# A fused decoder layer on one core: context and weights of the cross attention in fp32r parts, key and query stacks per group of four heads

## The chip, the cores and the metric

One Trainium2 chip, one of its cores. The metric is device time in microseconds (us) of one execution, lower is better. The kernel before took 1267.0 us (median of 3 runs, 1264.37 to 1269.11).

## What is computed

A batch of B = 8 sequences of T = 512 positions, width D = 256, float32. Three sublayers, each followed by a residual sum and a layer norm:

```python
x = _layernorm(x + _L0_attn_ref(x, ...))        # linear attention with decay 0.99, memory of 128
x = _layernorm(x + _L0_xattn_ref(x, ctx, ...))  # q from x; k, v from the context; 16 heads of 16, softmax
x = _layernorm(x + _L0_ffn_ref(x, ...))         # self attention, 16 heads, softmax, plus the experts:
# attn_out + moe_out
gate = _softmax(x @ W_gate + b_gate)            # 8 experts, the 2 largest gates kept, the others 0
expert_out = einsum('bsd,edf->bsef', x, W_experts) + b_experts
moe_out = einsum('bsef,bse->bsf', expert_out, combine)
```

## The kernel before

Both softmax attentions run through one pipeline. It passes over 16 phases: "C" (cross) and "S" (self) of the eight sequences, in the order C0, C1, S0, C2, S1 ... C7, S6, S7 (`PHASES`). A phase has four groups of four heads, so there are 64 groups, g = 0 to 63. A group takes four slots (one for each block of 128 keys), and a slot has two halves (one for each pair of heads). Slot s, half h is written (s, h) in the tables and step t = 2s + h in the loops. In a half-slot TensorE issues: the score matmuls of two heads (PSUM tile sc), two tiles whose row maxima are wanted six slots ahead (mx), in h = 0 the products of probabilities and values of the slot before (op), and in h = 1 what the tables put there, called units. ScalarE takes exp(sc) to probs, VectorE reduces each mx tile to maxima.

The row maxima come into the scores through two extra rows of the query stack: when a group's 16 max tiles are reduced, VectorE makes shift_n, TensorE transposes it (unit `shift`, in slot 4g-2, h = 1), VectorE copies it to shift_r, and SyncE (SP) sends two small DMAs `qs<-shift_r` into the stack (`shift(g)`, step 2(4g-2)+1). The first scores of the group, in slot 4g, wait for them on `shift_in`.

A stack (tiles ks and qs) holds three copies of a head's 16 rows (high, high, low parts against high, low, high). The `high` and `low` of a projection are the fp32r value and the rest: ScalarE writes the one, VectorE (`low`) the other into k_parts or q_parts. SP then sends six DMAs per stack (`stack`, L399), 128 KB each: one stack is half a phase (two groups, `HALF` = 4 heads deep on each side), in a ring of `RING` = 3. SP takes its DMAs in the order of the table OTHERS["sp"], each after its own waits, so a DMA that waits holds up all behind it.

Units go through two PSUM banks of tile ms, in turn: a unit may start only when the unit before the last one has been read out of its bank (`unit`, `wait_unit_out(pe, *ORDER[u - 2])`). For kc, qc, k3c, q3c it is VectorE's `low` that frees the bank, for `shift` the copy to shift_r, for most others a copy of ScalarE. The tables LIN_* place the units of the first two sublayers relative to the start of the C phase (kc0, kc1: keys of the context, two chunks; cv0, cv1: its values; qc: queries), MID_* those of the rest (k3c, q3c, v3a, v3b; x2T; gate; combT: transposes of the gates; be0, be1: gates times expert biases), MOE_* the 16 expert products. `heads` transposes a finished group's output in slot 4g+6, h = 1.

kc and cv are plain float32 products on ctxT_s, which SP loads whole into a tile of its own (L385). be0 and be1 are float32 products of combT (8 rows, kept in o1T) with the biases. k3c, q3c, v3 and the experts are already made from fp32r parts: three products (high by high, low by high, high by low) in one PSUM sum (`project_parts`, `project_part_rows`). The experts' results go ScalarE -> moe -> GpSimd, which adds them into x2.

Before the pipeline starts there are 23 slots of preparation for sequence 0 and 1 (LIN_FIRST, LIN_SECOND); the order of the queues there is written out at the start of each engine's block.

## Time and profile before

| | us |
|---|---|
| median of 3 runs | 1267.0 |
| the profiled execution's own time | 1266.94 |
| its span, first to last instruction | 1265.0 |
| TensorE matmul busy | 1220.8 (96%) |
| VectorE busy | 902.8 (71%) |
| ScalarE busy | 771.1 (61%) |
| GpSimd busy | 366.0 (29%) |

Matmuls are pipelined, so a busy time of TensorE adds up overlapping instructions and shows that it had work, not that it ran at its peak; what a unit costs is read from its start to the start of what follows. A float32 matmul stands in the trace as two instructions, an fp32r matmul as one. The steady part is the same from sequence to sequence, with a period of 149.3 us (two phases, 32 slots).

### The profile page before, as it was taken

The numbers are of one execution on the slowest core, as the hardware profiler recorded it, in microseconds if no ns is written. First come the engines' busy times: TensorE is split into PE (matmuls) and PEld (weight loads), VectorE is DVE, ScalarE is ACT, GpSimd is POOL, SyncE is SP. The second block draws the span as 40 slices with busy tenths as digits, with TensorE's granted clock in tenths as the row PEclk, the third lists the DMA queues.
The fourth block names the chain that finished last, engine by engine and source line by source line (L and its number), as shares of the span: only waits on it lengthen the run. The fifth ranks groups of instructions, "written<-read, shape, count | busy, mean of one in ns | idle before, by whom it ended". The sixth has DMA issues, their size and how long they took to land.

```text
span 1265.0 us, 19962 instructions
## 1 busy us (share of the span) xinstructions
PE 1220.8 (96%) x6936; PEld 601.8 (48%) x6936; DVE 902.8 (71%) x1836; ACT 771.1 (61%) x1072; POOL 366.0 (29%) x471
## 2 busy tenths in 40 slices
PE   8889999999999999999999999999999999999998
PEld 4433444544555445454554545454454534544443
DVE  2577886677777787777776777767877787667772
ACT  2255556666675765756657665666657576655664
POOL 6410103211621134320522206221153204430261
PEclk9899999999999999999999999999999999999999
DMA  7825034313233342233333143332223333303300
GB/s 254 135 43 94 18 52 68 51 29 76 50 69 52 51 85 42 51 45 70 68 67 61 20 74 68 68 52 45 51 42 51 52 52 52 68 2 52 52 19 18
DMA packets 50243, 74.92 MB, mean 59 GB/s; under 512 B 8536, under 2 KB 20320, under 8 KB 49888
## 3 DMA queue, kind: packets, MB, share of 16 engines
q1 hardware_dynamic: 48896, 72.72, 32.8%
q10 hardware_dynamic: 1248, 0.92, 0.4%
q8 instruction: 57, 0.93, 0.4%
q14 instruction: 42, 0.34, 0.1%
HBM read 18.04 MB, written 4.19 MB: 18 GB/s over the span
## 4 chain that ended last, share of the span: by engine, by line
PE 83%; DVE 7%; ACT 5%; issue 3%; DMA 1%; ACTq 0%; POOL 0%; SPq 0%; DVEq 0%
PE ms L451 38%; PE op L451 17%; PE sc L451 15%; PE mx L451 9%; DVE maxes L928 3%; ACT probs L759 2%; PE ms L557 2%; PE ms L502 1%; ACT moe L752 1%; PE ms L552 1%; DMA qs<-q_parts 1%; DMA w_ident<-in_ident 1%; DVE k_parts L838 0%; ACT x L777 0%; DVE heads L901 0%
## 5 line engine op out<-in xcount | busy, mean ns | idle before, releaser
L928 DVE TENSOR_REDUCE maxes<-mx 128x1 f32<-128x512 f32 x1024 | 657.4, 683 | 215.3 <-PE mx L451 213.4
L759 ACT ACTIVATE probs<-sc 128x1024 f32<-128x1024 f32 x512 | 524.3, 1024 | 373.8 <-PE sc L451 368.3
L1131 POOL TENSOR_TENSOR x<-x,moe 128x256 f32<-128x256 f32 x256 | 187.4, 732 | 687.0 <-ACT moe L752 666.5
L451 PE MATMUL op<-probs,v 128*32 128x512 f32 x2048 | 273.6, 606 | 2.9 <-ACT oT L697 2.5
L451 PE MATMUL sc<-qs,ks 50*128 50x512 f32 x1024 | 256.7, 497 | 11.9 <-ACT probs L759 10.3
L451 PEld LDWEIGHTS sc<-qs,ks 50*128 50x128 f32 x1024 | 95.4, 183 | 308.4 <-ACT probs L759 231.5
L451 PE MATMUL mx<-ks,qs 48*128 48x512 f32 x1024 | 209.0, 402 | 10.9 <-DVE maxes L928 8.9
L752 ACT ACTIVATE moe<-ms,comb 128x256 f32<-128x256 f32 x256 | 106.8, 472 | 22.1 <-PE ms L451 22.1
L451 PEld LDWEIGHTS mx<-ks,qs 48*128 48x128 f32 x1024 | 97.7, 187 | 20.8 <-DVE maxes L928 14.7
L451 PE MATMUL ms<-we_hi,x2T_hi 128*128 128x512 f32 x256 | 93.7, 447 | 2.5 <-DVE shift_r L892 1.3
L451 PEld LDWEIGHTS op<-probs,v 128*32 128x32 f32 x2048 | 40.5, 108 | 96.4 <-issue 95.0
L451 PE MATMUL ms<-we_hi,x2T_lo 128*128 128x512 f32 x256 | 80.5, 396 | 0.0
L451 PE MATMUL ms<-we_lo,x2T_hi 128*128 128x512 f32 x256 | 80.3, 394 | 0.0
L451 PEld LDWEIGHTS ms<-we_hi,x2T_hi 128*128 128x128 f32 x256 | 39.1, 188 | 35.4 <-issue 18.8
L451 PEld LDWEIGHTS ms<-we_lo,x2T_hi 128*128 128x128 f32 x256 | 48.0, 188 | 11.8
L451 PEld LDWEIGHTS ms<-we_hi,x2T_lo 128*128 128x128 f32 x256 | 48.0, 188 | 11.7
L838 DVE SCALAR_TENSOR_TENSOR k_parts<-ms,w_bk,k_parts 128x512 fp32r<-128x512 f32 x32 | 24.0, 751 | 33.7 <-ACT k_parts L698 33.3
L1093 POOL TENSOR_SCALAR var<-mv 128x4 f32<-128x4 f32 x24 | 5.5, 230 | 125.8 <-DVE mv L959 110.7
L557 PE MATMUL ms<-w_ident,oT 128*128 128x128 f32 x256 | 39.9, 279 | 1.8 <-DVE shift_r L892 1.0
L698 ACT ACTIVATE k_parts<-ms,w_bk 128x512 fp32r<-128x512 f32 x32 | 22.0, 687 | 32.1 <-PE ms L451 27.3
L844 DVE TENSOR_TENSOR v<-ms,w_bv 128x512 f32<-128x512 f32 x32 | 22.1, 690 | 27.2 <-PE ms L451 27.2
L557 PEld LDWEIGHTS ms<-w_ident,oT 128*128 128x128 f32 x256 | 29.5, 140 | 20.3 <-DVE shift_r L892 14.5
(131 smaller groups left out, 1264.8 us busy)
## 6 DMA issues: line engine op xcount, KB each, us to landing
ks<-k_parts SPq DMA_DIRECT2D x192, 128.0 KB, 4.2
qs<-q_parts SPq DMA_DIRECT2D x189, 128.0 KB, 4.6
xT_s<-in_xT SPq DMA_DIRECT2D x8, 512.0 KB, 3.8
x_s<-in_x SPq DMA_DIRECT2D x8, 512.0 KB, 4.0
ctxT_s<-in_ctxT SPq DMA_DIRECT2D x8, 512.0 KB, 4.2
out<-x SPq DMA_DIRECT2D x7, 512.0 KB, 2.9
qs<-shift_r SPq DMA_DIRECT2D x128, 8.0 KB
probs<-in_we SPq DMA_DIRECT2D x1, 1024.0 KB, 7.1
```

What stands on the lines that cost most here:

```text
L451: return nc.tensor.matmul(dst, lhsT, rhs, start=first, stop=last, skip_group_check=True)
L502: last = nc.tensor.transpose(bank[:, t * P:(t + 1) * P], src[:, t, c * P:(c + 1) * P], ident[:])
L552: last = nc.tensor.transpose(bank[0:SHIFT * HG * TB, 0:P], shift_n[:, n % 2].rearrange("p s a m -> p (s a m)"), ident[:])
L557: last = nc.tensor.transpose(bank[:, t * P:t * P + P], oT[:, t * P:t * P + P], ident[:])
L698: return nc.scalar.activation(dst, src, ACT.Identity, bias=bias, scale=1.0)
L752: nc.scalar.activation(moe[:, k % 2, j * D:j * D + D], bank[:, j * D:j * D + D], ACT.Copy, scale=comb[:, t, e:e + 1]).then_inc(moe_out, 1)
L759: nc.scalar.activation(probs[:, (2 * s + h) % 3, :, :], sc[:], ACT.Exp).then_inc(exp_out, 1)
L838: nc.vector.scalar_tensor_tensor(out=part[name][:, 1, :].bitcast(F32R), in0=unit_bank((task, n)), scalar=bias[:, c:c + 1], in1=part[name][ ...
L844: return nc.vector.tensor_tensor(dst[:, 2 * h:2 * h + 2, 0:H * VW].rearrange("p n (h d) -> p n h d", h=H)[:, :, :, 0:HD], unit_bank((task, ...
L928: nc.vector.tensor_reduce(maxes[:, g % 2, at:at + 1], mx[:, i % 3, :], AX_X, ALU.max).then_inc(max_out, 1)
L1093: nc.gpsimd.tensor_scalar(var[:, k, :], mv[:, k, :, 1], EPS, None, ALU.add).then_inc(step, 1)
L1131: nc.gpsimd.tensor_tensor(x2[:, n % 2, t, :], x2[:, n % 2, t, :], moe[:, k % 2, j * D:j * D + D], ALU.add).then_inc(acc, 1)
```

## The change

1. Keys and values of the cross attention are made of fp32r parts. The context comes raw into x1 (sequences 0 and 1) or x_s (from 2 on), ScalarE writes its high part (`ctx_high`), GpSimd the low one (`ctx_low`; for sequence 0 VectorE, `first_lows`). The weights wk2 and wv2 are loaded into x1b and split the same way at the start. kc0 and qc0 change places from sequence 2 on; kc0 of sequence 1 comes a slot earlier. The load of x for the next sequence goes behind `ctx_low`.
2. Stacks are per group: DMAs of half the size and twice as many, in a ring of five groups, and a semaphore for even and for odd groups. The second group's stack is issued at its own place in SP's order.
3. The expert bias is one fp32r product with 24 rows: VectorE builds comb3 (high, low, high parts of the gates; three more instructions in `choose_end`), and combT goes from (33, 1) to (34, 0) for sequences 1 to 6.
4. To make room: the value tiles v2 have 17 columns per head in place of 20, and above and tied lie in moe.

```diff
-VW = HD + 4
+VW = HD + 1
 SHIFT = 2
 SIDES = 2
-PAIRS = H // SIDES
-HALF = PAIRS // DC
-RING = 3
+WIDE = HG // SIDES
+RING = 5
...
-             "x1": (-16, 0), "qc0": (-15, 0), "cv1": (-15, 1), "kc1": (-14, 1), "qc1": (-7, 1),
+             "x1": (-16, 0), "qc0": (-15, 0), "cv1": (-15, 1), "kc1": (-14, 1), "qc1": (-6, 1),
...
-              "o1": (-2, 1), "y01": (-1, 1), "y23": (0, 1), "kc0": (2, 1), "x0": (4, 0), "x1": (5, 0), "qc0": (6, 1),
+              "o1": (-2, 1), "y01": (-1, 1), "y23": (0, 1), "kc0": (1, 1), "x0": (4, 0), "x1": (5, 0), "qc0": (6, 1),
...
-              "x_bias": (-4, 0), "x1_bias": (20, 1), "load_xT": (-4, 0), "load_x": (3, 0), "load_ctx": (12, 0)}
+              "x_bias": (-4, 0), "x1_bias": (20, 1), "load_xT": (-4, 0), "load_x": (3, 0), "load_ctx": (-15, 0),
+              "ctx_high": (-12, 1), "ctx_low": (-3, 0)}
...
-       "o1": (-23, 1), "y01": (-21, 0), "y23": (-20, 0), "x0": (-16, 0), "x1": (-15, 0), "kc0": (-14, 0),
-       "qc0": (-13, 1), "cv0": (-9, 1), "cv1": (-8, 1), "kc1": (-6, 0), "qc1": (-5, 1),
+       "o1": (-23, 1), "y01": (-21, 0), "y23": (-20, 0), "x0": (-16, 0), "x1": (-15, 0), "qc0": (-14, 0),
+       "kc0": (-13, 1), "cv0": (-9, 1), "cv1": (-8, 1), "kc1": (-6, 0), "qc1": (-5, 1),
...
-       "x_bias": (-27, 0), "x1_bias": (7, 0), "load_xT": (-31, 0), "load_x": (-17, 1), "load_ctx": (-1, 0)}
+       "x_bias": (-27, 0), "x1_bias": (7, 0), "load_xT": (-31, 0), "load_x": (-14, 1), "load_ctx": (-17, 1),
+       "ctx_high": (-15, 0), "ctx_low": (-15, 0)}
...
-            "gate": (29, 0), "gateT": (31, 0), "combT": (33, 1), "be0": (36, 0), "be1": (37, 0), "k3c0": (34, 0), "q3c0": (35, 1),
+            "gate": (29, 0), "gateT": (31, 0), "combT": (34, 0), "be0": (36, 0), "be1": (37, 0), "k3c0": (34, 0), "q3c0": (35, 1),
...
+        if n >= 1:
+            halves["sp"][lin_at("load_ctx", n)].append(("load_ctx", n))
+            halves["act"][lin_at("ctx_high", n)].append(("ctx_high", 0, n))
+            halves["pool"][lin_at("ctx_low", n)].append(("ctx_low", 0, n))
...
-                    halves["sp"][at(f"{name}{c}", n) + 1].append(("stack_" + kind, 2 * PHASE[layer, n] + c))
+                    t, g = at(f"{name}{c}", n), 4 * PHASE[layer, n] + 2 * c
+                    halves["sp"][t + 1].append(("stack_" + kind, g))
+                    halves["sp"][max(t + 1, 2 * 4 * (g + 1 - RING + 1) + 2) if g >= RING else t + 1].append(("stack_" + kind, g + 1))
...
-        ctxT_s = sb("ctxT_s", [P, DC, T])
+        ctxT_part = (sb("ctxT_hi", [P, DC, T]), sb("ctxT_lo", [P, DC, T]))
+        w2_part = {name: (sb(name + "_hi", [P, DC, D]), sb(name + "_lo", [P, DC, D])) for name in ("wk2", "wv2")}
...
+        comb3 = sb("comb3", [P, TB, TERMS * E])
+        be_part = sb("be_part", [TERMS * E, D])
+        be_stage = moe[0:TERMS * E, 1, 0:D]
...
+        def ctx_stage(n):
+
+            return (x1 if n < 2 else x_s)[:].rearrange("p n d -> p (n d)").rearrange("p (c t) -> p c t", c=DC)
...
+                    if n == 1:
+                        wait_unit(sp, "x0", 0)
+                        wait_unit(sp, "x1", 0)
+                        sp.wait_ge(x1b_out, TB)
+                    elif n >= 2:
+                        sp.wait_ge(ln_out[0], TB * (n + 1))
+                    sp.dma_start(ctx_stage(n), ctxT[n:n + 1].rearrange("o (c p) t -> p (o c) t", p=P)).then_inc(ctx_in, 16)
+
+            def stack(name, g):
...
+                first = 32 * (g % 2)
+                sp.wait_ge(part_low[name], g // 2 + 1)
+                if g == 0:
                     sp.wait_ge(fills, 5)
-                if e >= RING:
-                    sp.wait_ge(score, 2 * 8 * (e - RING + 1))
-                    sp.wait_ge(max_t, 32 * (e - RING + 1))
-                for side in range(SIDES if (name, e) != ("q", 0) else 1):
+                if g >= RING:
+                    sp.wait_ge(score, 2 * TB * (g - RING + 1))
+                    sp.wait_ge(max_t, HG * TB * (g - RING + 1))
+                for side in range(SIDES if (name, g) != ("q", 0) else 1):
                     for r in range(TERMS):
                         at = 64 * side + HD * r
-                        sp.dma_start(dst[at:at + HD, e % RING, :, :],
-                                     part[name][64 * side:64 * side + 64, which[r], :]).then_inc(stack_in[name], 16)
+                        src = 64 * side + first
+                        sp.dma_start(dst[at:at + HD, g % RING, :, :],
+                                     part[name][src:src + 32, which[r], :]).then_inc(stack_in[name][g % 2], 16)
...
-                    last = project(bank, W["wk2"], ctxT_s, slice(c * P, c * P + P))
+                    pe.wait_ge(ctx_low, DC * (n + 1))
+                    if n == 0:
+                        pe.wait_ge(w2_low, 2)
+                    last = project_parts(bank, w2_part["wk2"], ctxT_part, slice(c * P, c * P + P))
...
-                    last = project_rows(bank, D, ctxT_s, W["wv2"], slice(0, D), (2 * h, 2 * h + 1))
+                    pe.wait_ge(ctx_low, DC * (n + 1))
+                    if n == 0:
+                        pe.wait_ge(w2_low, 2)
+                    last = project_part_rows(bank, D, ctxT_part, w2_part["wv2"], slice(0, D), (2 * h, 2 * h + 1))
...
-                        last = nc.tensor.transpose(bank[0:E, t * P:t * P + P], comb[:, t, :], ident[:])
+                        last = nc.tensor.transpose(bank[0:TERMS * E, t * P:t * P + P], comb3[:, t, :], ident[:])
...
-                        last = mm(bank[:, j * D:j * D + D], combT[:, t * P:t * P + P], W["be"][:], True, True)
+                        last = mm(bank[:, j * D:j * D + D], combT[:, t * P:t * P + P].bitcast(F32R), be_part[:].bitcast(F32R),
+                                  True, True)
...
+            def context_high(n):
+                act.wait_ge(ctx_in, 16 * (n + 1))
+                if n >= 1:
+                    wait_unit(act, "kc1", n - 1)
+                    wait_unit(act, "cv1", n - 1)
+                for c in range(DC):
+                    copy(ctxT_part[0][:, c, :].bitcast(F32R), ctx_stage(n)[:, c, :]).then_inc(ctx_high, 1)
...
+                if t == lin_at("s23", 0):
+                    act.wait_ge(w2_in, 16 * 2)
+                    for name in w2_part:
+                        copy(w2_part[name][0][:].bitcast(F32R), w2_stage[name]).then_inc(w2_high, 1)
+                    context_high(0)
...
+            def first_lows():
+
+                for k, name in enumerate(w2_part):
+                    dve.wait_ge(w2_high, k + 1)
+                    nc.vector.tensor_tensor(w2_part[name][1][:].bitcast(F32R), w2_stage[name], w2_part[name][0][:],
+                                            ALU.subtract).then_inc(w2_low, 1)
+                for c in range(DC):
+                    dve.wait_ge(ctx_high, c + 1)
+                    nc.vector.tensor_tensor(ctxT_part[1][:, c, :].bitcast(F32R), ctx_stage(0)[:, c, :], ctxT_part[0][:, c, :],
+                                            ALU.subtract).then_inc(ctx_low, 1)
+
...
+                g_wait(COMB_STEP)
+                if n >= 1:
+                    wait_unit(dve, "combT", n - 1)
+                nc.vector.tensor_copy(comb3[:, :, 0:E].bitcast(F32R), comb[:]).then_inc(g_step, 1)
+                g_wait(COMB_STEP + 1)
+                nc.vector.tensor_tensor(comb3[:, :, E:2 * E].bitcast(F32R), comb[:], comb3[:, :, 0:E],
+                                        ALU.subtract).then_inc(g_step, 1)
+                nc.vector.tensor_copy(comb3[:, :, 2 * E:3 * E].bitcast(F32R), comb3[:, :, 0:E]).then_inc(g_step, 1)
...
+                elif task == "ctx_low":
+                    for c in range(DC):
+                        pool.wait_ge(ctx_high, DC * n + c + 1)
+                        nc.gpsimd.tensor_tensor(ctxT_part[1][:, c, :].bitcast(F32R), ctx_stage(n)[:, c, :], ctxT_part[0][:, c, :],
+                                                ALU.subtract).then_inc(ctx_low, 1)
```

Where it moves instructions. First TensorE, sequence 3, slots 33 and 34 relative to the start of its C phase. Before (comb is the transposes of unit combT, shift_n those of shift, oT those of heads, x2T_hi with w_hi the first part of k3c0):

```order
L451 MATMUL ms<-we_lo,x2T_hi 128x512 x2
L594 MATMUL ms<-w_ident,comb 8x128 x4
...
L552 MATMUL ms<-w_ident,shift_n 32x128
L451 MATMUL ms<-x2T_hi,w_hi 128x512 x2
L451 MATMUL ms<-x2T_lo,w_hi 128x512 x2
L451 MATMUL ms<-x2T_hi,w_lo 128x512 x2
L557 MATMUL ms<-w_ident,oT 128x128 x4
L451 MATMUL sc<-qs,ks 128x512 x2
```

and in the changed kernel:

```order
L473 MATMUL ms<-we_lo,x2T_hi 128x512 x2
...
L578 MATMUL ms<-w_ident,shift_n 32x128
L473 MATMUL ms<-x2T_hi,w_hi 128x512 x2
L473 MATMUL ms<-x2T_lo,w_hi 128x512 x2
L473 MATMUL ms<-x2T_hi,w_lo 128x512 x2
L620 MATMUL ms<-w_ident,comb 24x128 x4
L583 MATMUL ms<-w_ident,oT 128x128 x4
L473 MATMUL sc<-qs,ks 128x512 x2
```

combT now stands between k3c0 and heads, so the unit before the last one of heads is k3c0; before it was shift.

Second SP's queue around the second `shift` (group 1) at the start of the pipeline. Before:

```order
L376 DMA xT_s<-in_xT 128x2x512
L410 DMA qs<-shift_r 2x8x128 x4
L380 DMA x_s<-in_x 128x4x256
L399 DMA ks<-k_parts 16x4x512 x6
L410 DMA qs<-shift_r 2x8x128 x2
```

and in the changed kernel:

```order
L390 DMA xT_s<-in_xT 128x2x512
L429 DMA qs<-shift_r 2x8x128 x2
L420 DMA ks<-k_parts 16x2x512 x12
L429 DMA qs<-shift_r 2x8x128 x2
L396 DMA x_s<-in_x 128x4x256
```

The key stacks of groups 4 and 5 stand ahead of the shift of group 1; that of group 5 waits until all scores of group 0 are made.

Third SP's queue ahead of the shift of the first group of a C phase, here C2 (group 12; key and query stacks of groups 14 and 15, from kc1 and qc1 of sequence 2). Before:

```order
L399 DMA ks<-k_parts 16x4x512 x6
L399 DMA qs<-q_parts 16x4x512 x6
L410 DMA qs<-shift_r 2x8x128 x2
```

and in the changed kernel:

```order
L420 DMA ks<-k_parts 16x2x512 x6
L420 DMA qs<-q_parts 16x2x512 x6
L420 DMA ks<-k_parts 16x2x512 x6
L420 DMA qs<-q_parts 16x2x512 x6
L429 DMA qs<-shift_r 2x8x128 x2
```

From the query parts of qc1 on, 18 DMAs of stacks stand ahead of the shift in place of six.

## Rows read from the trace of the kernel before

**Rows 1.** The windows view, one steady period (busy us of each engine, granted clock)

```profile
432.59:581.93 149.34, 148.49 (x862) 73.71 (x862) 111.79 (x228) 95.95 (x135) 43.43 (x58) 1.00 0.34 58
```

**Rows 2.** Timeline of TensorE, units cv0 and kc1 (start us, us, line, operation)

```profile
557.85 1.89 PE L451 MATMUL ms<-w_wv,ctxT_s 128*128 128x256 f32 x8
559.67 0.50 PE L451 MATMUL sc<-qs,ks 50*128 50x512 f32 x2
...
571.70 1.88 PE L451 MATMUL ms<-ctxT_s,w_wk 128*128 128x512 f32 x4
...
573.42 0.60 PE L557 MATMUL ms<-w_ident,oT 128*128 128x128 f32 x4
```

**Rows 3.** The same view, q3c0 (from parts), be0, and two pieces of v3a

```profile
314.01 0.62 PE L451 MATMUL ms<-x2T_hi,w_hi 128*128 128x512 f32 x2
...
315.50 0.50 PE L451 MATMUL sc<-qs,ks 50*128 50x512 f32 x2
...
317.83 1.13 PE L451 MATMUL ms<-w_be,o1T 8*128 8x256 f32 x4
318.89 0.73 PE L451 MATMUL ms<-we_hi,x2T_hi 128*128 128x512 f32 x2
...
329.01 0.40 PE L451 MATMUL ms<-w_hi,x2T_lo 128*128 128x256 f32 x2
329.25 0.40 PE L451 MATMUL ms<-w_lo,x2T_hi 128*128 128x256 f32 x2
```

**Rows 4.** Timeline of all engines, slots 33 and 34 of sequence 3 (last: idle, releaser)

```profile
603.57 0.60 PE L594 MATMUL ms<-w_ident,comb 128*8 128x128 f32 x4
...
606.89 0.72 PE L451 MATMUL ms<-x2T_hi,w_hi 128*128 128x512 f32 x2 [0.17 <-ACT o1T L697]
...
608.40 0.60 PE L557 MATMUL ms<-w_ident,oT 128*128 128x128 f32 x4
...
608.66 0.69 ACT L698 ACTIVATE k_parts<-ms,w_bk 128x512 fp32r<-128x512 f32 x1 [0.91 <-PE ms L451]
...
609.38 0.75 DVE L838 SCALAR_TENSOR_TENSOR k_parts<-ms,w_bk,k_parts 128x512 fp32r<-128x512 f32 x1 [1.39 <-ACT k_parts L698]
```

**Rows 5.** The tile and source views: SP's time for one DMA (min/median/max ns)

```profile
L399 SPq DMA_DIRECT2D ks<-k_parts x192: 547/597/1104, 27.4 to 1178.2; - x192
...
L410 SPq DMA_DIRECT2D qs<-shift_r x128: 610/636/717, 62.9 to 1236.5; - x128
```

**Rows 6.** Timeline: query stack of qc1, and the scores that the next shift feeds

```profile
581.90 3.97 SPq L399 DMA_DIRECT2D qs<-q_parts  x6
...
595.11 0.50 PE L451 MATMUL sc<-qs,ks 50*128 50x512 f32 x2
```

**Rows 7.** The same at the start of C7 (group 52), with the shift

```profile
1029.83 3.75 SPq L399 DMA_DIRECT2D qs<-q_parts  x6
...
1037.85 16.30 SPq L410 DMA_DIRECT2D qs<-shift_r  x4
...
1040.60 0.50 PE L451 MATMUL sc<-qs,ks 50*128 50x512 f32 x2 [0.75 <-DMA qs<-shift_r]
```

**Rows 8.** The same at groups 6 and 60

```profile
164.37 3.75 SPq L399 DMA_DIRECT2D qs<-q_parts  x6
...
176.49 0.50 PE L451 MATMUL sc<-qs,ks 50*128 50x512 f32 x2
...
1179.58 3.75 SPq L399 DMA_DIRECT2D qs<-q_parts  x6
...
1192.48 0.50 PE L451 MATMUL sc<-qs,ks 50*128 50x512 f32 x2
```

**Rows 9.** Timeline of TensorE: last scores of group 0, first of group 1

```profile
81.62 0.50 PE L451 MATMUL sc<-qs,ks 50*128 50x512 f32 x2
...
84.22 0.51 PE L451 MATMUL sc<-qs,ks 50*128 50x512 f32 x2
```

**Rows 10.** Windows: after the thin start, and around the wait of rows 7

```profile
74.00:79.00 5.00, 4.63 (x19) 1.42 (x18) 3.27 (x8) 3.40 (x5) 1.49 (x4) 0.66 0.01 3
...
1030.00:1060.00 30.00, 27.22 (x191) 12.60 (x195) 25.00 (x55) 19.14 (x27) 4.50 (x5) 1.00 0.31 48
```

**Rows 11.** Timeline of TensorE: the first max tiles

```profile
43.11 0.50 PE L451 MATMUL mx<-ks,qs 48*128 48x512 f32 x2 [2.01 <-DMA qs<-q_parts]
```

**Rows 12.** The page's groups: weight loads of the value products

```profile
L451 PEld LDWEIGHTS op<-probs,v 128*32 128x32 f32 x2048 | 40.5, 108 | 96.4 <-issue 95.0
```

More of the change, by code:

```diff
@@ L265, in decoder @@
         o1T = sb("o1T", [P, T])
-        combT = o1T[0:E, :]
+        combT = sb("combT", [TERMS * E, T])[:]
         gateT = sb("gateT", [P, P])[:]
@@ L272, in decoder @@
         part = {n: sb(n + "_parts", [P, 2, T]) for n in "qk"}
-        qs = sb("qs", [P, RING, HALF, T])
-        ks = sb("ks", [P, RING, HALF, T])
+        qs = sb("qs", [P, RING, WIDE, T])
+        ks = sb("ks", [P, RING, WIDE, T])
         v2 = [sb(f"v2_{n}", [P, TB, H * VW + 32 - VW]) for n in range(2)]
@@ L295, in decoder @@
         g_p = sb("g_p", [P, TB, E])
-        above = sb("above", [P, TB, E, E])
-        tied = sb("tied", [P, TB, E, E])
         rank = sb("rank", [P, TB, E])
@@ L300, in decoder @@
         moe = sb("moe", [P, 2, 512])
+        above, tied = (moe[:, 0, k * TB * E * E:(k + 1) * TB * E * E].rearrange("p (n e f) -> p n e f", n=TB, e=E) for k in range(2))
+        comb3 = sb("comb3", [P, TB, TERMS * E])
+        be_part = sb("be_part", [TERMS * E, D])
+        be_stage = moe[0:TERMS * E, 1, 0:D]
         we_part = (sb("we_hi", [P, DC, E * D]), sb("we_lo", [P, DC, E * D]))
@@ L305, in decoder @@
         W3_COLS = (slice(0, 2 * D), slice(2 * D, 3 * D))
+        w2_stage = {name: x1b[:, 2 * k:2 * k + 2, :] for k, name in enumerate(w2_part)}
         we_stage = (probs[:].rearrange("p s h t -> p (s h t)")[:, 0:E * D],
@@ L402, in shift @@
             def shift(g):
                 sp.wait_ge(shift_out, g + 1)
-                wide = HG // SIDES
-                first = wide * (g % 2)
                 for side in range(SIDES):
                     at = 64 * side + ROWS
-                    rows = SHIFT * wide * TB
-                    sp.dma_start(qs[at:at + SHIFT, stack_of(g) % RING, first:first + wide, :]
+                    rows = SHIFT * WIDE * TB
+                    sp.dma_start(qs[at:at + SHIFT, g % RING, :, :]
                                  .rearrange("a h (n t) -> a (h n) t", n=TB),
@@ L705, in high @@
                 if e >= 1:
-                    act.wait_ge(stack_in[name], 16 * TERMS * SIDES * e)
+                    for signal in stack_in[name]:
+                        act.wait_ge(signal, 16 * TERMS * SIDES * e)
                 wait_unit(act, task, n)
@@ L735, in take_out @@
                     wait_unit(act, task, n)
-                    copy(combT, bank[0:E, :]).then_inc(done, 1)
+                    copy(combT.bitcast(F32R), bank[0:TERMS * E, :]).then_inc(done, 1)
                 elif task in ("be0", "be1"):
@@ L770, in other @@
                         act.wait_ge(x1b_out, TB * n)
+                    if k == 0 and n < 2:
+                        act.wait_ge(ctx_low, DC * (n + 1))
                     if k == 1 and n == 0:
@@ L1053, in _ @@
                     dve.wait_ge(w3_cut, 4)
+                    dve.wait_ge(be_in, 16)
+                    nc.vector.tensor_copy(be_part[:].bitcast(F32R), be_stage).then_inc(be_cut, 1)
+                    dve.wait_ge(be_cut, 1)
+                    nc.vector.tensor_scalar(be_stage, be_stage, W["side"][:, 0:1], None, ALU.mult).then_inc(be_cut, 1)
+                    dve.wait_ge(be_cut, 2)
+                    nc.vector.scalar_tensor_tensor(out=be_part[:].bitcast(F32R), in0=be_part[:], scalar=W["side"][:, 1:2],
+                                                   in1=be_stage, op0=ALU.mult, op1=ALU.add).then_inc(be_cut, 1)
                 units = UNITS.get(t - 1, [])
@@ L1198 @@
         "we": by_chunk(arr(ffn + "W_experts").transpose(1, 0, 2).reshape(D, E * D)),
-        "be": arr(ffn + "b_experts"),
+        "be": np.tile(arr(ffn + "b_experts"), (TERMS, 1)),
+        "side": np.repeat(np.array([[0, 1], [0, 1], [1, -1]], np.float32), E, 0),
         "ident": np.eye(P, dtype=np.float32),
```

83 lines of the change are left out of this document (47 added, 36 removed).

## The prediction

> **What bounds the kernel now.** I read the windows of a steady period first. In 149.34 us TensorE has work for 148.49, VectorE for 111.79, ScalarE for 95.95, GpSimd for 43.43 [rows 1]. So TensorE's queue is the bound: what is taken out of it is won, and a wait put into it is lost, whatever the others do. Then I read its timeline for the price of the units that the change touches, the waits of the places where it moves something, and SP's queue, which is idle most of the time but feeds the scores of every group through `shift`. The sum is made against the profiled execution, 1266.94 us with a span of 1265.0, as good as the median of 1267.0. A measurement tells 0.5% (6.3 us) from no change: the bounds are 1260.7 and 1273.3.
>
> **Products from parts, less time.** A plain float32 kc takes 571.70 to 573.42, 1.72 us, a cv 557.85 to 559.67, 1.82 us [rows 2]. The like unit from parts, q3c0 (six instructions of 512 columns, the shape of the new kc), takes 314.01 to 315.50, 1.49 us. In v3a pairs of 256 columns start 0.24 apart (329.01, 329.25), so the new cv with 12 instructions takes 6 x 0.24 plus about 0.06, 1.50 us [rows 3]. That gives 0.23 per kc and 0.32 per cv, 1.1 us per sequence. For sequence 0 these units lie before the pipeline, under other waits, and I count nothing: 7 x 1.1 = 7.7 us. be0 now takes 317.83 to 318.89, 1.06 us [rows 3]; after it there are two instructions of 256 columns, 0.24 and some 0.1 of entry. 0.72 less, 16 times: 11.5 us. Together -19.2. combT's transposes keep their four instructions (24 columns are loaded in place of 8).
>
> The Trainium skill (FP8 and Floating Point Precision, TensorE Precision Notes) has true FP32 as four passes through the array, so kc from three products would take three quarters. By that a kc and a cv would save 0.43 to 0.46 instead of 0.23 and 0.32, 4.7 us more over seven sequences. The units of the same shape in this trace save less, and the rows decide.
>
> **Work on the other engines.** The split of the context costs ScalarE two copies and GpSimd two subtractions per sequence at slot -15; ScalarE has 53 us free in a period and GpSimd 106 [rows 1], and kc0 comes 2.5 slots (over 10 us) later. Nothing. If GpSimd's part were late, kc0 would wait on TensorE and all behind it; I leave that to the range. At the start, the added copies and subtractions fall into stretches in which ScalarE and VectorE wait for o1 and y01: nothing.
>
> **combT behind k3c0: a new wait.** Banks alternate, so heads waits until the unit before the last one has been read out. Before, that is shift, long read: heads follows k3c0 at 608.40 at once. Now it is k3c0, and its bank is free only when ScalarE has made the high part (608.66) and VectorE the low (609.38 plus 0.75 = 610.13) [rows 4]. The moves up to k3c0's end about cancel (combT's 0.6 and the 0.17 wait gone from before it, against VectorE's three more instructions in front of the max tiles), so k3c0 ends at about the same time as before, and heads starts at 610.2 in place of 608.40: +1.8 us. It stands in sequences 1 to 6: +10.8. Behind heads in TensorE's queue are the scores of the next slot, and nothing hides it.
>
> **Twice as many stack DMAs: shifts come late.** One stack DMA costs SP 0.6 us, a shift DMA of 8 KB 0.64 [rows 5]. The size makes no difference there, so I take 0.625 (3.75 for six) for the half-sized ones too. Ends: 0.3, if the cost went with the bytes, and 0.8 with an odd long one. The key and query stacks of a second half (kc1, qc1) now stand with 18 DMAs between the query's low part and the shift, before with six. 18 x 0.625 = 11.25, the shift's two 1.3, and its landing: at 1037.85 the shift was issued, ended by 1039.15, and the scores began at 1040.60 on it, so 1.4 [rows 7]. The scores can begin 13.95 us after the query stack's first DMA.
> - Group 28: 581.90 + 13.95 = 595.85 against 595.11 [rows 6]: 0.75 us. The same at the start of C2 to C6, five times: 3.7.
> - Group 52: 1029.83 + 13.95 = 1043.8 against 1040.60 [rows 7]: 3.2.
> - Groups 6 and 60: 178.3 against 176.49 and 1193.5 against 1192.48 [rows 8]: 1.8 and 1.0. Group 58 has the same queue as 6, and I take 1.8: together 4.6.
> - Group 1: the ring wait `if g >= RING` is not in the place of the stack of group 5 (g is 4 there), so SP waits with that stack until the last scores of group 0, at 81.62 plus 0.5, then six DMAs (3.75), the shift (1.3) and the landing (1.4): 88.6 against 84.22, of which cv0 is done 0.3 sooner [rows 9]: 4.7.
>
> Sum of shifts: 16.2 us, all in TensorE's queue.
>
> **Start.** The first max tile waits for q_parts at 43.11 [rows 11]. Its data are now half. On the other side the whole key stacks and a context load come ahead of it. I estimate 1.5 us less; ends 0 and 3.
>
> **Clock.** In 74 to 79 us the granted clock averages 0.66 of the full 2.4 GHz, so it was at its lower level of 1.2 GHz for most of it, after slots in which TensorE waited time and again; around a wait of 0.75 us in a dense part it stays at 1.00 [rows 10]. After the two long waits (4.7 and 3.2) I count a few us at half clock, 1.5 us together.
>
> The Trainium skill (TensorE: Matmul & The Clock Gate, Part 1) says that the throttled state is the default and activity releases it. That speaks against every wait that the change adds; with the long ones the trace agrees, with the short one not.
>
> **Sum.** -19.2 + 10.8 + 16.2 - 1.5 + 1.5 = +7.8 us, 1274.7 against the run of 1266.94: I forecast 1275, slower by 0.6%.
>
> **Rivals.**
> - **SP's issue goes with the size** (the other side). If a half-sized DMA costs 0.3 us, the 18 take 5.4 and all waits but that of group 1 are gone (it keeps 4.7 - 6 x 0.32 = 2.8). Sum -19.2 + 10.8 + 2.8 - 1.5 + 0.3 = -6.8: 1260, just faster. It decides below about 0.35 us per DMA. For it: nothing; against it: 8 KB and 128 KB cost the same [rows 5]. 0.12. Halfway (0.45) gives about 1264, no change: 0.05.
> - **The wait of heads is covered**: VectorE and ScalarE get to k3c0 sooner than rows 4 say, or the time comes back in the next slots. Then 1275 - 10.8 = 1264. TensorE has only 0.85 us without work in a period [rows 1], so I see no slack that could give it back. 0.20, no change.
> - **Shifts land later**, queued behind the stacks' data: two to three us more at each of ten places, 1295 at most, 1285 in the middle. For it: the transfers now stand directly ahead of the shift. Against: SP issues 64 KB in 0.625 us, half the rate of before. 0.13, slower.
> - **Value tiles of 17 columns**: the 2048 weight loads take 108 ns each [rows 12]. If the odd row width made each value product 5 ns longer, +10 us: 1285. No row shows it. 0.05, slower.
> - **Half clock after every wait**: ten waits, each with some 3 us of work at half speed, +1.5 us each, +13.5 beyond what is counted: 1288. Against it stands the short wait of rows 10. 0.05, slower. [...]
> - **Products at three quarters**: a kc or cv 0.2 or 0.14 us shorter than in rows 3, 1275 - 4.7 = 1270. Against: q3c0 has the shape. 0.02, no change. (So by the four passes of the Trainium skill, cited above.)
>
> **How the numbers follow.** The forecast has what is left, 0.38. With the three later cases (0.23) that is 0.61 for more than 1273.3 us; but the forecast lies only 1.7 us above that bound, and I give 0.11 of it to no change. Slower 0.50. No change: 0.11 + 0.20 + 0.05 + 0.02 = 0.38. Faster: 0.12. The 80% range goes from the first rival to the middle of the later ones: 1260 to 1286.
>
> **What would show it.** In the profile after: kc and cv units of 1.5 us, be of 0.35; SP's ks and qs issues still near 0.6 us, 384 and 381 of them; TensorE idle before heads' transposes, with VectorE's k_parts as releaser, 1 to 2 us, six times; score matmuls released by DMA qs<-shift_r, the longest at 84 to 89 us and at the start of C7; the steady period 149.3 - 1.1 - 1.4 + 1.8 + 0.75, near 149.3. Wrong if SP's issues are at 0.3 us, if heads does not wait, or if the period falls below 148.

## The result and the profile after

The changed kernel takes 1304.9 us, median of 4 runs (1301.7 to 1309.1), against 1267.8 before: ratio 1.0299, 95% interval 1.0262 to 1.0336, slower. The forecast was 1275 and the range ended at 1286: the direction was right, the size was off by 30 us. The profiled execution took 1306.02 us with a span of 1304.2, so it can be set against the span of 1265.0 before.

The page of the changed kernel: busy times, the granted clock in 40 slices, the chain that ended last by engine and by line, the groups of score and max matmuls with the idle time ahead of them, and the stack issues.

```profile
PE 1226.5 (94%) x7000; PEld 613.6 (47%) x7000; DVE 920.0 (71%) x1867; ACT 779.6 (60%) x1090; POOL 381.7 (29%) x485
...
PEclk9689998999999999999999999999999999999999
...
PE 71%; SPq 11%; DVE 7%; ACT 4%; issue 4%; DMA 3%; POOL 0%; ACTq 0%; DVEq 0%
...
L473 PE MATMUL sc<-qs,ks 50*128 50x512 f32 x1024 | 259.7, 503 | 34.6 <-DMA qs<-shift_r 22.9
```

SyncE's queue is now in the chain that ended last (SPq 11%), and the scores waited 22.9 us for the shift, 13 times; before it was one wait of 0.75 us. The views that answer to the forecast's sources, first the source views of SyncE's issues [rows 5] (min/median/max ns):

```profile
L420 SPq DMA_DIRECT2D ks<-k_parts x384: 558/592/1816, 27.4 to 1224.5; - x192
L420 SPq DMA_DIRECT2D qs<-q_parts x381: 558/592/1612, 37.2 to 1228.4; - x191
```

Half the bytes, the same 0.59 us at the median, as the forecast took it; single issues took up to 1.8 us. Then the timeline at group 28 [rows 6]: two issues of six stack DMAs and a third stand between the first query stack and the shift.

```profile
603.13 3.73 SPq L420 DMA_DIRECT2D qs<-q_parts  x6
606.97 4.44 SPq L420 DMA_DIRECT2D ks<-k_parts  x6
611.52 3.73 SPq L420 DMA_DIRECT2D qs<-q_parts  x6
615.30 1.32 SPq L429 DMA_DIRECT2D qs<-shift_r  x2
...
618.01 0.50 PE L473 MATMUL sc<-qs,ks 50*128 50x512 f32 x2 [1.59 <-DMA qs<-shift_r]
```

The shift lands 1.39 us after its issue has ended (616.62), as forecast. The two longest waits, of group 1 [rows 9] and of group 52 [rows 7], and the pieces of the first max tiles' timeline [rows 11]:

```profile
42.80 0.50 PE L473 MATMUL mx<-ks,qs 48*128 48x512 f32 x2 [4.26 <-DMA qs<-q_parts]
...
95.57 0.80 PE L473 MATMUL sc<-qs,ks 50*128 50x512 f32 x2 [3.59 <-DMA qs<-shift_r]
...
1071.57 0.79 PE L473 MATMUL sc<-qs,ks 50*128 50x512 f32 x2 [4.16 <-DMA qs<-shift_r]
```

Timeline at slot 34 of sequence 3 [rows 4]: heads' transposes wait for the low part of k3c0 and not for their own operand.

```profile
631.81 0.61 PE L620 MATMUL ms<-w_ident,comb 128*24 128x128 f32 x4
631.99 0.69 ACT L725 ACTIVATE k_parts<-ms,w_bk 128x512 fp32r<-128x512 f32 x1 [1.41 <-PE ms L473]
...
632.71 0.75 DVE L885 SCALAR_TENSOR_TENSOR k_parts<-ms,w_bk,k_parts 128x512 fp32r<-128x512 f32 x1 [0.95 <-ACT k_parts L725]
...
633.51 0.66 PE L583 MATMUL ms<-w_ident,oT 128*128 128x128 f32 x4 [1.10 <-DVE k_parts L885]
634.10 0.50 PE L473 MATMUL sc<-qs,ks 50*128 50x512 f32 x2
```

Windows of the changed kernel: the start, and the stretch behind the wait of group 52 (columns as in [rows 1]; the granted clock is the last but two).

```profile
44.00:68.00 24.00, 21.60 (x40) 9.45 (x40) 12.32 (x23) 3.24 (x6) 16.61 (x10) 0.51 0.44 110
...
1071.00:1082.00 11.00, 9.74 (x36) 3.60 (x37) 7.18 (x19) 4.70 (x6) 0.00 (x0) 0.53 0.01 2
```

TensorE has work for nine tenths of both and runs at its lower level of 1.2 GHz, called half clock below. Added up from the clock's record, it was there for 64.9 us of the execution, against 11.6 us before. The four runs of the changed kernel order themselves by it: 1309.1 us at a mean granted clock of 0.973, 1306.0 at 0.975, 1303.8 at 0.979, 1301.7 at 0.987.

**Where the time went.** I set the start of each group's first scores against before (after minus before, as steps from group to group):

| place | step, us | forecast |
|---|---|---|
| group 0, the start | +8.0 | -1.5 |
| groups 1 and 2 | +5.9 | +4.7 |
| groups 6 to 8 | +4.7 | +1.8 |
| groups 12, 20, 28, 36, 44 | +7.6 | +3.7 |
| groups 40, 48, 56 | +1.5 | 0 |
| slots 33 to 35, seen at groups 13, 21, ..., 53 | +16.7 | +10.8 |
| groups 52, 58 to 60 | +8.2 | +6.0 |
| all others, the shorter units | -13.5 | -19.2 |
| sum | +39.1 | +6.3 and 1.5 for the clock |

No place is new except groups 8, 40, 48 and 56; each term came out worse than forecast. What the experiments have to tell is why.

### The profile page after: what moved, and what is told of

It reads as the page before. It is cut to its first block, busy times and chain, and to the rows that moved or that the text cites. A ratio compares the mean times of both kernels' runs of the same rounds, so it can differ in the third digit from the quotient of the medians.

```text
span 1304.2 us, 20667 instructions
## 1 busy us (share of the span) xinstructions
PE 1226.5 (94%) x7000; PEld 613.6 (47%) x7000; DVE 920.0 (71%) x1867; ACT 779.6 (60%) x1090; POOL 381.7 (29%) x485
## 4 chain that ended last, share of the span: by engine, by line
PE 71%; SPq 11%; DVE 7%; ACT 4%; issue 4%; DMA 3%; POOL 0%; ACTq 0%; DVEq 0%
PE ms L473 31%; PE op L473 14%; PE sc L473 13%; SPq L420 10%; PE mx L473 8%; DVE maxes L975 3%; PE ms L583 2%; DMA qs<-shift_r 2%; PE ms L524 2%; ACT probs L789 1%; DVE q_parts L885 1%; ACT q_parts L725 1%; PE ms L578 1%; DVE k_parts L885 1%; SPq L429 1%
## 5 line engine op out<-in xcount | busy, mean ns | idle before, releaser
L473 PE MATMUL sc<-qs,ks 50*128 50x512 f32 x1024 | 259.7, 503 | 34.6 <-DMA qs<-shift_r 22.9
L473 PE MATMUL mx<-ks,qs 48*128 48x512 f32 x1024 | 213.6, 411 | 14.8 <-DVE maxes L975 10.5
L473 PEld LDWEIGHTS mx<-ks,qs 48*128 48x128 f32 x1024 | 100.4, 191 | 26.6 <-DVE maxes L975 13.5
L885 DVE SCALAR_TENSOR_TENSOR k_parts<-ms,w_bk,k_parts 128x512 fp32r<-128x512 f32 x32 | 24.0, 750 | 24.7 <-ACT k_parts L725 23.9
L724 ACT ACTIVATE oT<-op 128x512 f32<-128x512 f32 x64 | 38.3, 599 | 1.4 <-PE op L473 1.4
```

Source lines behind the costliest of these rows:

```text
L473: return nc.tensor.matmul(dst, lhsT, rhs, start=first, stop=last, skip_group_check=True)
L724: return nc.scalar.activation(dst, src, ACT.Copy)
L885: nc.vector.scalar_tensor_tensor(out=part[name][:, 1, :].bitcast(F32R), in0=unit_bank((task, n)), scalar=bias[:, c:c + 1], in1=part[name][ ...
```

## The experiments

Each edit is on the changed kernel unless said otherwise; kernel 5 is the kernel of run 5, and so on. Times are ratios to runs of the kernel before on the same chip; 1% is 12.7 us.

**1. qc1 back in its slot.**

```
-             "x1": (-16, 0), "qc0": (-15, 0), "cv1": (-15, 1), "kc1": (-14, 1), "qc1": (-6, 1),
+             "x1": (-16, 0), "qc0": (-15, 0), "cv1": (-15, 1), "kc1": (-14, 1), "qc1": (-7, 1),
```

> The changed kernel with the product qc1 of sequence 0 back in slot -7, ahead of the first max tiles, as before the change; nothing else. Theory (clock): the first scores are 8.0 us late because TensorE stood 4.3 us for the first stack, the granted clock fell and stayed at 0.5 for 23.9 us; with qc1 in the hole the wait falls to about 2 us, the half clock to about 7 us, the first scores come at 67 to 69 us, and the time is 1296 to 1300 us. Rival (queue): the stacks and the context load ahead on SyncE's queue make the start late whatever TensorE does; then the first scores stay at 73 to 75 us and the time at 1303 to 1306 us.

Measured: 1300.4 us, ratio 1.0239 (1.0216 to 1.0262). The wait of the first max tiles is 1.0 us, the half clock 6.8 us, the first scores stand at 69.15 us. That looks like the theory, but runs 3, 4 and 11 get to the same place without the edit (below), and run 12, which is run 3 with this edit added, is no faster than run 3 (1.0188 against 1.0179). What qc1 gains ahead of the first max tiles is lost behind them. ScalarE, VectorE and TensorE in this kernel:

```profile
44.77 1.14 ACT L724 ACTIVATE ctxT_hi<-x 128x512 fp32r<-128x512 f32 x2
45.81 0.68 ACT L725 ACTIVATE q_parts<-ms,bq2s 128x512 fp32r<-128x512 f32 x1
...
46.52 0.75 DVE L885 SCALAR_TENSOR_TENSOR q_parts<-ms,bq2s,q_parts 128x512 fp32r<-128x512 f32 x1 [1.23 <-ACT q_parts L725]
...
47.92 0.80 PE L473 MATMUL mx<-ks,qs 48*128 48x512 f32 x2 [2.04 <-DVE maxes L975]
```

The added copies of the context stand on ScalarE ahead of qc1's high part; VectorE waits 1.23 us for it with the max reductions queued behind, and TensorE 2.04 us for those.

**2. TensorE kept busy in front of the first max tiles.**

```
+                if s == -MAX_LEAD and h == 0:
+                    busy(5, T)
```

> The changed kernel with five filling products of 512 columns on TensorE just ahead of the first max tiles (about 4.3 us at full clock, the length of the wait there), qc1 left in slot -6. Theory (clock): the clock does not fall, or is back soon, the first scores come at 66 to 69 us, the time is 1296 to 1300 us. Rival (queue): first scores at 73 to 76 us, time 1303 to 1308 us. A third way: the place of qc1 behind the first max tiles costs by itself (its bank and ACT behind it), then the clock is full and the first scores are still later than 70 us.

Measured: 1300.7 us, ratio 1.0246 (1.0224 to 1.0267), first scores at 71.34 us. The clock fell all the same, 6.8 us, later. That is outside the ranges of both theories, and the first scores are later than in three of the four kernels without filling (68.76 to 74.82 us, below). Filling bought nothing that can be told from run 1, and the clock theory of the start has no support here.

**3. combT back in slot 33.**

```
-            "gate": (29, 0), "gateT": (31, 0), "combT": (34, 0), "be0": (36, 0), ...
+            "gate": (29, 0), "gateT": (31, 0), "combT": (33, 1), "be0": (36, 0), ...
```

> The changed kernel with the transpose of the combine weights back in slot 33 second half; nothing else. Theory (two banks): the heads unit waits no longer for the low part of k3c0, the 1.1 us waits go in all six middle sequences, and so does what follows them; time 6 to 11 us less than the changed kernel, 1294 to 1299 us. Rival (VectorE): the three more VectorE instructions at the end of the choice make the transpose itself wait in slot 33 for as long, and the step from slot 33 to 35 stays 2.3 to 2.9 us above before; time 1302 to 1305 us.

Measured: 1291.2 us, ratio 1.0179 (1.0155 to 1.0204), 1.2% off the changed kernel. Timeline of TensorE at the same slot:

```profile
617.98 0.60 PE L620 MATMUL ms<-w_ident,comb 128*24 128x128 f32 x4 [0.60 <-DVE comb L1115]
618.50 0.50 PE L473 MATMUL sc<-qs,ks 50*128 50x512 f32 x2
...
622.35 0.63 PE L473 MATMUL ms<-x2T_hi,w_lo 128*128 128x512 f32 x2
622.81 0.60 PE L583 MATMUL ms<-w_ident,oT 128*128 128x128 f32 x4
623.34 0.50 PE L473 MATMUL sc<-qs,ks 50*128 50x512 f32 x2
```

Both theories have a part. heads waits no longer, and the step at slots 33 to 35 falls by 1.73 to 2.36 us in five middle sequences and by 1.02 in the sixth. But the transpose now waits 0.60 us for VectorE's last combine instruction, and 0.52 to 0.55 us of the step stays (3.09 in the sixth, where the half clock of group 52's wait lies in it). The time fell by more than the 6 to 11 us expected: of the 15.2 us between the two profiles these steps are 11.0, and the start is 4.7.

**4. Odd groups' stacks behind the shift.** SyncE's queue alone:

```
-  ... max(t + 1, 2 * 4 * (g + 1 - RING + 1) + 2) if g >= RING else t + 1
+  ... max(t + 1, 2 * 4 * (g + 1 - RING + 1) + 6) if g + 1 >= RING else t + 1
```

> The changed kernel with the stacks of every odd group issued four half slots later, behind the shift that they stood ahead of, and group 5's stacks held to the same rule; nothing else. Theory (queue): the 13 waits of the scores for the shift (22.9 us in all) are the 0.62 us per issue of twelve stack transfers ahead of it; they fall under 3 us in all, and the half clock behind the two longest (groups 1 and 52) goes too; the time is 1274 to 1284 us. Rival (landing): the shift lands late since many small transfers are in flight, then the waits stay above 10 us in all and the time above 1292 us. Rival (buffers): the later stacks make ACT's copies of the next products wait for the stacks, the max tiles then wait for stacks, and the time stays above 1295 us with waits named after the parts.

Measured: 1288.6 us, ratio 1.0152 (1.0137 to 1.0167). All 13 waits for the shift are gone, so they were the queue. The time did not come down to the 1274 to 1284 us expected, because the load of the next context now stood behind those stacks. Timelines of SyncE, ScalarE and TensorE:

```profile
370.55 1.31 SPq L429 DMA_DIRECT2D qs<-shift_r  x2
371.98 4.25 SPq L420 DMA_DIRECT2D ks<-k_parts  x6
376.34 4.83 SPq L420 DMA_DIRECT2D qs<-q_parts  x6
381.21 0.58 SPq L404 DMA_DIRECT2D x_s<-in_ctxT  x1
...
385.19 1.15 ACT L724 ACTIVATE ctxT_hi<-x_s 128x512 fp32r<-128x512 f32 x2 [3.16 <-DMA x_s<-in_ctxT]
...
387.30 0.50 PE L473 MATMUL sc<-qs,ks 50*128 50x512 f32 x2 [3.17 <-ACT probs L789]
```

ScalarE waits for the context, the exponentials are queued behind that copy, and TensorE waits for them, in five periods (10.7 us in all). It is the same fault at another place: an urgent transfer behind twelve that have time.

Runs 3 and 4 leave the start as the changed kernel has it, and their first scores stand at 70.12 and 68.99 us, not at 74.82.

**5. All three edits** (runs 1, 3 and 4 together, the stacks five half slots later to pass the context's load).

> The changed kernel with all three edits at once: qc1 of sequence 0 back in slot -7, the transpose of the combine weights back in slot 33, and the odd groups' stacks behind the shift and behind the load of the next context (five half slots later than in the changed kernel, group 5's too). Theory (three added waits on top of a true saving): the ratios of the single edits add up (0.6%, 1.2%, 1.5% off 1.030), and the 13 us of waits for the context that the late stacks made are not there; the time is 1248 to 1258 us, below the kernel before by 1 to 1.6%. Rival (no saving): the cheaper products gave back their time elsewhere, and without the waits the time is that of before, 1265 to 1272 us.

Measured: 1282.6 us, ratio 1.0099 (1.0073 to 1.0125). A miss of both ranges: in the half slot that they now share, the stacks are still issued ahead of the load (11.4 us of waits for the context), and group 5's k stacks came so late that ScalarE waited for them (1.9 us, and 4.7 us at group 3).

**6. The expert bias in plain fp32 again**, on kernel 5.

```
-                        last = mm(bank[...], combT[:, t * P:t * P + P].bitcast(F32R), be_part[:].bitcast(F32R), True, True)
+                        last = mm(bank[...], combT[:, t * P:t * P + P], be_part[:], True, True)
```

> As the kernel with all three edits, with the expert bias's 16 x 2 products in plain fp32 again (over 24 rows, the same sum), nothing else. The prediction's price: 0.72 us per unit, 16 units, 11.5 us more than with all three edits. Rival (hidden): the units lie in slots that end on another engine, then it is 0 to 4 us.

Measured: 1284.5 us, ratio 1.0100 (1.0057 to 1.0143), 1.9 us above kernel 5 and not to be told from it: by time alone the rival's 0 to 4 us fits and the forecast's 11.5 does not. The timelines show what the unit itself does. With parts (kernel 5), and below it in fp32:

```profile
783.87 0.50 PE L473 MATMUL ms<-be_part,combT 24*128 24x256 f32 x2
784.30 1.13 PE L473 MATMUL ms<-x1T 128*128 128x512 f32 x2
```

```profile
785.97 1.13 PE L473 MATMUL ms<-be_part,combT 24*128 24x256 f32 x4
787.03 1.12 PE L473 MATMUL ms<-x1T 128*128 128x512 f32 x2
```

The unit takes 0.43 us in place of 1.06 [rows 3]; 0.63 us less where I had 0.72. Of it the scores show 0.40 us behind be0 and 0.48 behind be1 in sequences 1 to 5, 1.02 for both in sequence 6, 5.4 us together. So the term was too large; the time shows still less of it, and the waits for the context, which move the steps by up to 3.2 us at one place between these two profiles, hide how much.

**7. k and v of the context as one fp32 product of the high parts**, on kernel 5; it leaves out both products with low parts.

```
-                    last = project_parts(bank, w2_part["wk2"], ctxT_part, slice(c * P, c * P + P))
+                    last = project(bank, w2_part["wk2"][0], ctxT_part[0], slice(c * P, c * P + P))
```

and the like for v. 

> As the kernel with all three edits, with the products of k and v of the context as one plain fp32 product of the high parts, as many columns and as long as in the kernel before; it leaves out the two products with the low parts. The prediction's price: 0.23 us for each kc and 0.32 us for each cv unit, 7.7 us more than with all three edits (1.1 us per sequence). Rival (hidden): 0 to 2 us.

Measured: 1286.9 us, ratio 1.0125 (1.0076 to 1.0173). The intervals of 5 and 7 overlap (4.3 us between the medians, 7.7 forecast), but the steps of the scores are 0.30, 0.31, 0.30 and 0.31 us for the four units of a period, 1.2 us per sequence where I had 1.1. By the steps this term was right.

**8. The kernel before, with combT in slot 34**, and nothing else.

```
-            "gate": (29, 0), "gateT": (31, 0), "combT": (33, 1), "be0": (36, 0), ...
+            "gate": (29, 0), "gateT": (31, 0), "combT": (34, 0), "be0": (36, 0), ...
```

> The kernel before with one entry changed: the transpose of the combine weights in slot 34 first half, behind k3c0. Theory (two banks): the heads unit of slot 34 waits for k3c0's low part on VectorE, 1.1 us in each of the six middle sequences, and the scores of the slot behind it are 1.8 to 2.4 us later than before; time 7 to 14 us more than before. My prediction's own price was 1.8 us x 6 = 10.8 us. Rival: the wait is taken up by slack in the next slot, time within 3 us of before.

Measured: 1276.7 us, ratio 1.0044 (1.0021 to 1.0068), 5.6 us, a little under the 7 to 14 expected. The step is 1.25 to 1.29 us in five sequences and 1.48 in one, 7.8 us together. So moving the transpose alone costs 1.3 each, not my 1.8.

**9. The queue put right.** Kernel 5 with SyncE's order mended:

```
-  ... 2 * 4 * (g + 1 - RING + 1) + 7) if g + 1 >= RING else t + 1
+  ... 2 * 4 * (g + 1 - RING + 1) + (2 if g == 4 else 7 if g % 8 == 2 else 6)) if g + 1 >= RING else t + 1
+    for tasks in halves["sp"].values():
+        tasks.sort(key=lambda task: 0 if task[0] == "shift" else 1 if task[0] == "load_ctx" else 2)
```

> The changed kernel with qc1 of sequence 0 in slot -7, the combine transpose in slot 33, the odd groups' stacks behind the shift (group 5's in slot 5, the others' at least four half slots later than in the changed kernel), and the load of the next context ahead of the stacks of its half slot. Theory: what was left in the kernel with all three edits were waits of ScalarE for the context (1.5 to 3.2 us in each of five periods, 11.5 us in all) and for group 5's k stacks (4.7 us at group 3); both go, and the time is 1262 to 1268 us, 0 to 0.6% below before. Rival (landing): the context is waited for however early its load is issued, or the q stacks issued behind it are waited for instead; the time stays at 1275 to 1283 us.

Measured: 1263.3 us, ratio 0.9962 (0.9939 to 0.9984), as the theory has it: without its three added waits the change saves 0.4%. The timelines of SyncE at two places: shift ahead of the stacks, and the context ahead of them; then the windows view of the steady period.

```profile
589.17 1.31 SPq L431 DMA_DIRECT2D qs<-shift_r  x2
590.60 3.76 SPq L422 DMA_DIRECT2D ks<-k_parts  x6
594.47 3.74 SPq L422 DMA_DIRECT2D qs<-q_parts  x6
```

```profile
371.69 0.38 SPq L406 DMA_DIRECT2D x_s<-in_ctxT  x1
372.51 3.95 SPq L422 DMA_DIRECT2D ks<-k_parts  x6
```

```profile
410.63:558.32 147.69, 146.23 (x870) 73.68 (x869) 113.21 (x230) 96.68 (x136) 45.94 (x60) 1.00 0.24 59
```

A period of 147.7 us against 149.3 before and 151.1 in the changed kernel (slot 84 to slot 116, 488.30 to 639.43). No score waits for a shift, and no copy for a context. The half clock takes 18.0 us in all.

**10. The parts of the combine weights on GpSimd**, on kernel 9: the three instructions moved from VectorE.

```
-                nc.vector.tensor_copy(comb3[:, :, 0:E].bitcast(F32R), comb[:]).then_inc(g_step, 1)
+                    nc.gpsimd.tensor_copy(comb3[:, :, 0:E].bitcast(F32R), comb[:]).then_inc(g_step, 1)
...
```

> As the kernel just described, with the three parts of the combine weights made on GpSimd instead of VectorE. Theory (VectorE's order): the scores of slot 34 are 0.55 us later than before in each middle sequence because three more VectorE instructions (0.5 us) stand ahead of the max reductions; the step goes, 3 to 4 us less. Rival: GpSimd is slower and the transpose in slot 33 waits for it; 0 to 6 us more.

Measured: 1261.9 us, ratio 0.9954 (0.9929 to 0.9978), the same as kernel 9 by its interval. The step that it was to remove grew from 0.55 to 0.79 us, and the six waits of the transposes from 3.6 to 5.0 us in all, so my theory of it fell: it is the time until the combine weights are there that counts, and GpSimd is slower. Why the time is no worse stays open; the two kernels differ by half-clock pieces at other places.

**11. Only the condition for group 5.**

```
-  ... if g >= RING else t + 1
+  ... if g + 1 >= RING else t + 1
```

> The changed kernel with the condition of the stacks' place holding for group 5 too (its stacks in slot 5 instead of slot 2, behind shift 1); nothing else. Theory (ring): the 3.6 us wait of group 1's scores goes, and so does the half clock of some 7 us behind it (2.5 us at group 2); 5 to 6.5 us less than the changed kernel, 1298 to 1300 us. Its first part is the changed kernel's own, so its first scores are one more draw of the start: if 74.8 us belongs to the change they come at 73 to 76 us, if it was the clock's draw of one execution, at 69 to 71 us as in two of the kernels with other edits. Rival: the wait moves to group 2's shift, less than 2 us gained.

Measured: 1298.0 us, ratio 1.0251 (1.0204 to 1.0298). Group 1's wait falls from 3.59 to 1.25 us, and the steps of groups 1 and 2 by 3.8 and 2.8 us, 6.6 in all. The first scores stand at 68.76 us. In the changed kernel SyncE had issued both key stacks without a stop:

```profile
85.14 7.63 SPq L420 DMA_DIRECT2D ks<-k_parts  x12
```

So what the edit took away from in front of the shift was six issues; a standstill of SyncE for the ring does not show. The six of group 4's stack still stand there.

**12. Everything mended but the queue** (runs 1 and 3 together; it differs from kernel 9 in SyncE's order alone).

> The changed kernel with qc1 of sequence 0 in slot -7 and the combine transpose in slot 33, and SyncE's queue as in the changed kernel. It differs from the kernel of 1263 us in SyncE's order alone. Theory (the queue is the largest term): 12 to 13 waits of the scores for the shift, 19 to 23 us in all, and some us of half clock behind the longest; 1286 to 1291 us, 23 to 28 us above that kernel. The prediction's own price of the queue was 16.2 us, which would give 1279 to 1280 us. Rival (the edits overlap): the waits at the queue are partly the same time as the waits at the heads unit; then 1272 to 1279 us.

Measured: 1292.1 us, ratio 1.0188 (1.0161 to 1.0215), 2.26% or 28.7 us above kernel 9, just above the range. The waits for the shift are ten, 22.0 us in all. The two traces are 33.5 us apart (the profiled executions lie 2.1 us above and 2.7 below their medians), with 58.5 us at half clock against 18.0. The windows view from the first scores to the end, kernel 12 and then kernel 9:

```profile
68.78:1292.41 1223.63, 1167.32 (x6808) 581.69 (x6807) 886.04 (x1807) 760.41 (x1062) 346.24 (x454) 0.98 0.21 51
...
69.50:1258.89 1189.39, 1150.03 (x6808) 573.95 (x6807) 885.17 (x1807) 759.59 (x1062) 345.66 (x454) 1.00 0.22 53
```

Of the 34.2 us TensorE is idle for 17.0 (56.3 against 39.4) and busy for 17.3 more with the same 6808 matmuls. Idle time grows by less than the 22.0 us of waits for the shift, since other waits of TensorE (for maxima and combine weights) are shorter in kernel 12.

## Why the forecast was wrong

**What was right.** That TensorE's queue is the bound and little hides a wait in it; SyncE's 0.6 us per DMA, whether of 8, 64 or 128 KB; the landing of 1.4 us; group 5's stack ahead of the shift of group 1 (3.6 us of wait, 4.7 forecast); all the shift waits that were named; heads behind k3c0; k and v of the context (run 7). The rival "issue goes with the size" was rightly small, and value tiles of 17 columns cost nothing (weight loads 108 ns as in [rows 12]).

**The two terms that failed most are the shifts' 16.2 us and the clock's 1.5: together 17.7, and the queue cost 28.7 (run 12), 33.5 by the two traces.** The waits were forecast in the right places. Their steps add up to 21.2 us where I had 16.2, and groups 40, 48 and 56, which I did not name, add 1.5. Group 1 came out below its forecast (3.4 for 4.7) and group 52 near it (3.4 for 3.2; its wait of 4.16 us holds the 0.75 that it had before). The others were too small: 7.6 for 3.7 at the starts of C2 to C6, 2.3 and 3.2 for 1.8 at groups 6 and 58, 1.3 for 1.0 at group 60.

The step of the prediction that failed here is the queue's length, "18 x 0.625 = 11.25", and with it the 13.95 us from the first query stack to the scores. At groups 52 and 60, where every issue took 0.59 us, it was 14.2 us, for each change of tile costs 0.1. At the other ten places, where single issues took 0.7 to 1.6 us, it was 14.3 to 15.2 (14.88 at group 28: a stack of six took 4.44 us there). [rows 6] shows such a stack, 3.97 us for six, and I took 3.75. Where a wait was forecast at 0.75, one more microsecond more than doubles it.

The rest is the clock. I gave it only to the two longest waits, 1.5 us. In kernel 12 TensorE spends 40.5 us more at its lower level than in kernel 9, and is busy 17.3 us longer with the same matmuls (run 12). By the medians, 28.7 us in place of 33.5, the clock's part would be some 12 us, an estimate that leaves the 17.0 us of idle time as they are. The rival "half clock after every wait" was priced at 13.5 us beyond what is counted, 15.0 in all, and had 0.05; by size it was nearly this, though not every wait has it: in kernel 12 seven of the ten do, and those of 0.49, 0.95 and 1.46 us do not. That the short wait of [rows 10] cost nothing was no evidence for the others: it stood alone in a dense stretch. In the changed kernel a wait of 1.41 us (group 36) is followed by half clock and one of 1.59 us (group 28) is not; why is open.

The Trainium skill (TensorE: Matmul & The Clock Gate, Part 1) says that the throttled state is the default and that activity releases it. The traces agree in this: behind waits of 3.6 and 4.2 us come 6.8 and 10.2 us at 1.2 GHz, and where the waits were taken away (runs 4 and 9) those stretches are gone.

**heads, 10.8 us forecast, 16.7 measured.** The place was right, the sum was not. Where no half clock falls into them (run 4) the six steps are 2.26 to 2.33 us, 13.9 together; the other 2.8 us go with half clock. Run 8 has the move alone at 1.3 us per sequence, so 1.8 was too much for it. The step that failed is "the moves up to k3c0's end about cancel": with the transpose in its old slot VectorE's three more instructions leave 0.55 us (kernel 9), and both together cost 2.3 us, 0.5 more than their sum. Why they cost more together is open. In the changed kernel two of the steps are 2.9 and one is 4.1 us, the last with the half clock of group 52's wait in it.

**The start, -1.5 us forecast, +8.0 in the profile.** Most of that was one draw. With the same program up to there the first scores came at 74.82, 70.12, 68.99 and 68.76 us in four kernels (the changed one, runs 3, 4 and 11), with 23.9, 10.2, 10.2 and 6.8 us at half clock ahead of them; before it was 6.8. These are single executions and not all on one chip, so chip and execution are not told apart. What belongs to the change is +1.9 to +3.3 us against 66.85, and kernel 9 has it too (+2.65). I priced only the stacks, and there "half the data" and "the whole key stacks ahead" did about cancel: the first max tiles begin at 42.5 to 43.5 us as before (43.11), though SyncE issues the query stack at 37.20 in place of 33.19. What I left out is that qc1 moves behind them. In kernel 11 it stands there from 45.79 to 48.93, partly at half clock, where before it filled the hole. And with qc1 back (run 1) ScalarE's context copies, "nothing" in my text, take its place. This last is read from the trace of run 1; no kernel was run without those copies.

**The savings, 19.2 us forecast, 13.5 seen.** k and v gave what was forecast (run 7). The bias gave 0.9 to 1.0 us per middle sequence and not 1.44 (run 6): the unit takes 0.43 us, not 0.34, and part of the rest is time in which the next unit waits anyway (0.15 us for q_parts in front of the expert product behind be0). The bias units of sequences 0 and 7, 2.9 us in the forecast, lie in groups that the table has in other rows.

## What to carry to other kernels

When a change splits transfers, count the issues and not the bytes, and write down what else stands in that queue: here 0.59 us of SyncE per piece turned a saving of 0.4% (kernel 9) into a loss of 1.9% (kernel 12), and the order of the queue, the urgent ones (the shift, the next context) ahead of those with time, is all the difference between the two. In this kernel the waits of the engine that bounds it were paid nearly twice, once as waits and once as the slower clock behind them; price the second from a kernel that has such waits, not from a lone one. And before one believes a difference at the start of a profile, look at the same stretch in a second execution.

## What was not expected of the hardware

- The time at half clock behind the same code differs from execution to execution: 23.9, 10.2, 10.2 and 6.8 us at the start of four kernels that are the same up to there, worth up to 6 us of time; the four ran on more than one chip.
- Five fp32 products of 512 columns in front of the first max tiles did not save the start (run 2): the clock stayed up behind them and fell at 61.6 us instead, for 6.8 us.
- At TensorE's wait of 1.7 us for oT in slot 29 (group 7; 201.42 us in the kernel before) the kernel before keeps its clock. Nine of the twelve profiles with the change show 3.4 to 6.8 us at half clock there (6.8 us in the changed one, and with it the step of 2.0 us at group 8), and so does run 8, the kernel before with one unit moved (a step of 2.7 us). What tips it is open.
